# Third block of a two-block transformer pair: the MLP's up products split into two halves of 256 tokens

## The chip, the cores and the metric

The kernel runs on one core of one Trainium2 chip. The metric is the device time of one execution in microseconds (us). A core has engines that run side by side, each with its own instruction queue: TensorE (PE; its weight loads are shown apart as PEld), VectorE (DVE), ScalarE (ACT), GpSimd (POOL) and SyncE (SP), which here only issues DMAs. They wait for each other on semaphores.

## The reference

The input `x` is 32 sequences of 128 tokens by 512 features, float32. Two layers follow each other; the second is cut here to what matters:

```python
    def _L1_cond_ref(x, cond, ...):
        ...
        x_in = x
        h = film(rmsnorm(x, norm1_w), cond, film1_w, film1_b)
        Q = h @ q_w + q_b
        K = h @ k_w + k_b
        V = h @ v_w + v_b
        scores = jnp.einsum('bnd,bmd->bnm', Q, K) * D ** (-0.5)
        attn = jax.nn.softmax(scores, axis=-1)
        out = jnp.einsum('bnm,bmd->bnd', attn, V)
        x = x_in + (out @ proj_w + proj_b)
        x_in = x
        h = film(rmsnorm(x, norm2_w), cond, film2_w, film2_b)
        h = jax.nn.gelu(h @ mlp_w1 + mlp_b1, approximate=False) @ mlp_w2 + mlp_b2
        return x_in + h
```

Before it, layer 0 is an attention with 16 heads between two conditioned layer norms. The change touches `h @ mlp_w1` alone: 4096 tokens by 512 features, times a 512 by 2048 weight.

## The kernel before

The program has three blocks, one after the other on every engine: layer 0 (to about 568 us), the attention half of layer 1 (to about 847 us), and the MLP half of layer 1, the third block, to the end. Tokens are worked in tiles of `P` = 128 and groups of `GB` = 4 tiles, so `GT` = 512 tokens and `NG` = 8 groups. The helper `groups` (line 71) writes a block's body for the first group, once more as a hardware loop over the six groups between, and for the last.

Products of float32 values are made of rounded operands. A value is split into a high part, rounded to the type float32r, and a low part, the rounded rest; `split_product` (lines 567 to 571) issues three matmuls for one product: high by high (L569), high by low (L570) and low by high (L571). Its second and third arguments are the stationary operand, which PE loads as weights ahead of each matmul, and the next two are the one that streams through. All of them add into one PSUM bank of 128 partitions by 512 columns.

In the third block the streaming operand of an up product is the normed input of a group, `hc_hi` and `hc_lo`, features on partitions and 4 chunks (`C`) of 512 tokens each. These two tiles lie where the second block had `hb_hi` and `hb_lo`, and the trace shows them under those names; the weights `w1_hi` and `w1_lo` are `w_hi` and `w_lo` in it, and `g_hi`, `g_lo` are the gelu's result. Names behind the arrow stand in the order streamed, loaded: `bank<-hb_hi,w_hi` is an up matmul, `bank<-w_hi,g_hi` a down matmul.

PE's order is written out by hand in `body_c`. For each group `g` it runs `FT` = 16 up products `up(g, f)`, each 4 chunks x 3 = 12 matmuls, into `bank[f % 2]`. From the fourth on, each is followed by a down product `down(g, f - LAG)` of the piece three before (`LAG` = 3), also 12 matmuls, 3 for each of the four token tiles, into banks 2 to 5. Three down products are left over at the end of a group; into the first two of them `norm_c` puts eight transposes of the next group's tokens (L970). ACT applies the gelu to each up bank (L1257), and DVE splits its result into `g_hi` and `g_lo`.

The next group's `hc_hi` and `hc_lo` are made from the transposes: tiles 0 and 2 by DVE (L1658, L1663, L1280), tiles 1 and 3 by ACT (L1052, L1245), with the low halves of all four on DVE, in the order 0, 1, 2, 3. Each low half raises the semaphore `clo` by one. `body_c` waits for `clo` to reach `GB * g` before `up(g, 0)`. Each up product ends with one count of `up_done`, for which ACT's gelu waits; PE waits for `gelu_done` before it writes a bank again.

Of the kernel before, what the change touches and what calls it, by code (L numbers as in the profile page):

```python
# [11 lines left out]
P = 128  # L12
D = 512
C = D // P
NB = 32
GB = 4
GT = GB * P
# [19 lines left out]
def wait(engine, sem, value):  # L37

    if isinstance(value, int) and value <= 0:
        return  # L40
    engine.wait_ge(sem, value)
# [37 lines left out]
def block_pair_kernel(nc, xt, cond_t, cols_d, bp0_d, bv0_d, pb1_d, b2_d, wg_t, wb_t, wqkv, wp0,  # L79
                      film1, film2, wq1_t, wk1_t, wv1_t, wp1, w1, w2, out):  # L80
    with ExitStack() as ctx:
# [140 lines left out]
        w1_hi = run("w1_hi", [P, C, FF], F32R)  # L222
        w1_lo = run("w1_lo", [P, C, FF], F32R)
# [4 lines left out]
        hc_hi, hc_lo, xc, xnc = hb_hi, hb_lo, xb, xnb  # L228
# [17 lines left out]
        bank = [ctx.enter_context(nc.psum_tensor(f"bank{i}", [P, D], F32)) for i in range(8)]  # L246
# [14 lines left out]
        def sem(name):  # L261
            return ctx.enter_context(nc.semaphore(name))
# [59 lines left out]
        chi_act, chi_dve, clo = sem("chi_act"), sem("chi_dve"), sem("clo")  # L322
# [243 lines left out]
        def _(pe):  # L566
            def split_product(dst, w_hi, w_lo, a_hi, a_lo, start, stop):

                nc.tensor.matmul(dst, w_hi, a_hi, start=start, stop=False)  # L569
                nc.tensor.matmul(dst, w_hi, a_lo, start=False, stop=False)  # L570
                return nc.tensor.matmul(dst, w_lo, a_hi, start=False, stop=stop)  # L571
# [3 lines left out]
            for k in range(C):  # L575
                if k % 2 == 0:
                    pe.wait_ge(wgb_in[k // 2], 32)
                for i in range(2):
                    tile = 2 * (k % 2) + i
                    last = nc.tensor.matmul(ps_s[0][NB * tile:NB * (tile + 1), :], cond[:, k, :], wgb[:, i, k, :],  # L580
                                            start=(k < 2), stop=(k >= 2))
# [3 lines left out]
            for c in range(C):  # L585
                last = nc.tensor.transpose(ps_s[1][:, c * P:(c + 1) * P], fv0[:, c * P:(c + 1) * P], ident[:])
# [13 lines left out]
            for i in range(2):  # L600
                for c in range(C):
                    last = nc.tensor.transpose(ps_t[i][0:NB, c * P:(c + 1) * P], st_flat[:, i * C + c, :], ident[:])
# [165 lines left out]
            for t in range(NB):  # L768
                g, b = t // GB, t % GB
# [81 lines left out]
            for c in range(C):  # L851
                last = nc.tensor.transpose(bank[3][:, c * P:(c + 1) * P], uc_rows[:, c * P:(c + 1) * P], ident[:])
# [46 lines left out]
            def transpose_pb(g, b):  # L899
                t = GB * g + b  # L900
                pe.wait_ge(bexp, t + 1)
                wait(pe, bpt, 2 * (t - 1))
                nc.tensor.transpose(ps_t[b % 2][:, 0:P], pb[:, b % 2, :], ident[:]).then_inc(btp, 1)

            def attend_b(g, b):
                t = GB * g + b
                pe.wait_ge(bpt, 2 * t + 2)
                pe.wait_ge(bg_free[0], bank_uses_b(g, 4 + 2 * b) + 1)
                wait(pe, x2_ready, t - 1)
                split_product(bank[6 + b % 2][:], ptb_hi[:, b % 2, :], ptb_lo[:, b % 2, :], vb_hi[:, b, :],  # L910
                              vb_lo[:, b % (GB - 1), :], True, True).then_inc(bpv, 1)
# [51 lines left out]
            def norm_c(g, b):  # L963

                t = GB * g + b
                pe.wait_ge(cxn, t + 1)

                wait(pe, ct_free_act if b % 2 else ct_free_dve, 2 * g + b // 2)
                for c in range(C):
                    last = nc.tensor.transpose(bank[6 + b % 2][:, c * P:(c + 1) * P], xnc[:, b, c * P:(c + 1) * P],  # L970
                                               ident[:])
                last.then_inc(ct_full, 1)
# [5 lines left out]
            def up(g, f):  # L978
                n = FT * g + f
                wait(pe, gelu_done, n - 1)  # L980
                for k in range(C):
                    last = split_product(bank[f % 2][:], w1_hi[:, k, f * P:(f + 1) * P], w1_lo[:, k, f * P:(f + 1) * P],
                                         hc_hi[:, k, :], hc_lo[:, k, :], k == 0, k == C - 1)
                last.then_inc(up_done, 1)

            def down(g, f, first):
                n = FT * g + f
                if first and f % 2 == 0:
                    pe.wait_ge(w2_hi_made, f // 2 + 1)
                    pe.wait_ge(w2_lo_made, f // 2 + 1)  # L990
                pe.wait_ge(g_hi_ready, n + 1)
                pe.wait_ge(g_lo_ready, n + 1)
                if f == 0:
                    wait(pe, y_ready, GB * g)
                for b in range(GB):
                    tok = slice(b * P, (b + 1) * P)
                    last = split_product(bank[2 + b][:], g_hi[:, f % (LAG + 1), tok], g_lo[:, f % (LAG + 1), tok],
                                         w2_hi[:, f, :], w2_lo[:, f, :], f == 0, f == FT - 1)
                    if f == FT - 1:
                        last.then_inc(acc_done, 1)  # L1000
                if f < FT - 1:
                    last.then_inc(down_done, 1)

            def body_c(g, first, last):

                if first:
                    pe.wait_ge(blo, NB + GB)
                wait(pe, clo, GB * g)
                if first:

                    pe.wait_ge(w1_hi_made, 2 * C - 2)
                    pe.wait_ge(w1_lo_made, 2 * C - 2)
                for f in range(FT):
                    if first and f == FT // 2:
                        pe.wait_ge(w1_hi_made, 2 * C)
                        pe.wait_ge(w1_lo_made, 2 * C)
                    up(g, f)
                    if first and f == 0:
                        transpose_pb(NG - 1, GB - 1)
                    if first and f == 1:  # L1020
                        attend_b(NG - 1, GB - 1)
                    if f >= LAG:
                        down(g, f - LAG, first)
                if first:
                    pe.wait_ge(x2_ready, NB)
                for f in range(FT - LAG, FT):
                    if not last and f < FT - LAG + 2:
                        for b in range(2):
                            norm_c(g, 2 * (f - (FT - LAG)) + b)
                    down(g, f, first)  # L1030

            groups(pe, body_c)


# [844 lines left out]
```

## Time and profile before

| | |
|---|---|
| median of 3 runs | 1560.82 us (1558.15 to 1561.24) |
| the profiled execution | 1561.84 us, its span 1560.1 us |
| mean granted TensorE clock | 0.995 |
| PE busy | 1524.7 us, 98% of the span, 8992 matmuls |
| PE weight loads (PEld) | 1237.5 us, 79%, beside the matmuls |
| DVE, ACT, POOL busy | 786.5, 597.0, 578.1 us |

The span is the time from the first to the last instruction that the profile shows. PE's busy time counts pipelined matmuls, which overlap each other: a matmul of 0.39 us may be followed by the next after 0.23 us. So the distance from start to start, not the length, tells what one costs. The clock is given as a share of full speed, 1.00 being 2.4 GHz.

### The profile page before, as it was taken

Reading aid. Unit: us, or ns where it says so; the run is one execution under the profiler, and the core shown is the slowest. Engines: PE = TensorE matmul, PEld = TensorE weight load, DVE = VectorE, ACT = ScalarE, POOL = GpSimd, SP = SyncE. Lnnn points to the kernel's source line nnn. Section 1 sums busy time; section 2 is a strip of 40 time slices with the busy share of each in tenths; the row PEclk is TensorE's granted clock in tenths of the full one; section 3 lists DMA queues with packets and bytes.
Section 4 is the critical chain, followed back from the end, with each engine's and each line's share of the span. In section 5 each row is a group of like instructions: output and inputs, shape, how many; then the busy total and the mean of one; then the engine's idle time right before and its main releaser. Section 6 shows DMA issues by size and latency. Waiting matters only on the chain.

```text
span 1560.1 us, 25120 instructions
## 1 busy us (share of the span) xinstructions
PE 1524.7 (98%) x8992; PEld 1237.5 (79%) x8992; DVE 786.5 (50%) x1616; ACT 597.0 (38%) x1884; POOL 578.1 (37%) x504
## 2 busy tenths in 40 slices
PE   5999999999999998999999999999999999999999
PEld 3888888888887666778787888888888888888887
DVE  5667777777776665444546533242423324242522
ACT  4656565655543444555555321121212212121210
POOL 5666666767553534443333402121120202121100
PEclk9999999999999999999999999999999999999999
DMA  7122222222216234222223402020101102020100
GB/s 248 62 80 85 82 89 92 79 96 69 81 56 239 88 113 161 84 81 87 87 101 144 147 1 82 0 74 7 67 13 46 34 0 81 0 74 7 54 1 28
DMA packets 56577, 117.72 MB, mean 75 GB/s; under 512 B 6288, under 2 KB 6288, under 8 KB 55984
## 3 DMA queue, kind: packets, MB, share of 16 engines
q1 hardware_dynamic: 56496, 116.65, 21.8%
q8 instruction: 49, 0.80, 0.2%
q14 instruction: 32, 0.26, 0.1%
HBM read 91.33 MB, written 25.30 MB: 75 GB/s over the span
## 4 chain that ended last, share of the span: by engine, by line
PE 91%; DMA 3%; DVE 2%; ACT 1%; POOL 1%; issue 1%; SPq 1%; ACTq 0%; DVEq 0%; POOLq 0%
PE bank L569 26%; PE bank L571 25%; PE bank L570 25%; PE bank L648 4%; PE bank L641 2%; PE bank L659 2%; PE bank L944 1%; PE bank L691 1%; PE bank L593 1%; DMA xb<-x_dram 1%; PE bank L970 1%; PE bank L700 1%; DMA xa<-xt_in 1%; ACT hb_new L1052 1%; POOL xa L1733 1%
## 5 line engine op out<-in xcount | busy, mean ns | idle before, releaser
L1257 ACT ACTIVATE gf<-bank,cols 128x512 f32<-128x512 f32 x128 | 88.3, 690 | 513.2 <-PE bank L571 513.1
L1692 DVE CAST g_hi<-gf 128x512 fp32r<-128x512 f32 x128 | 67.7, 529 | 426.5 <-ACT gf L1257 426.4
L1092 ACT ACTIVATE pa<-bank,neg_max 128x128 f32<-128x128 f32 x512 | 181.7, 409 | 135.0 <-DVE neg_max L1364 135.0
L569 PE MATMUL bank<-w_hi,g_hi 128*128 128x512 f32 x512 | 200.5, 392 | 0.0
L569 PE MATMUL bank<-hb_hi,w_hi 128*128 128x512 f32 x512 | 199.4, 389 | 0.6 <-issue 0.6
L571 PE MATMUL bank<-w_hi,g_lo 128*128 128x512 f32 x512 | 199.4, 389 | 0.0
L570 PE MATMUL bank<-w_lo,g_hi 128*128 128x512 f32 x512 | 199.2, 389 | 0.0
L571 PE MATMUL bank<-hb_hi,w_lo 128*128 128x512 f32 x512 | 199.2, 389 | 0.0
L570 PE MATMUL bank<-hb_lo,w_hi 128*128 128x512 f32 x512 | 199.2, 389 | 0.0
L1742 POOL TENSOR_TENSOR xrc<-xrc,b 128x512 f32<-128x512 f32 x32 | 48.1, 1533 | 302.6 <-DMA xrc<-x_dram 302.6
L1768 POOL TENSOR_TENSOR pa<-pa,rec 128x512 f32<-128x512 f32 x128 | 132.2, 1041 | 49.8 <-DVE rec L1387 49.7
L1757 POOL TENSOR_TENSOR rstd<-ve,neg_half 128x1 f32<-128x1 f32 x64 | 41.0, 640 | 283.9 <-DVE ve L1446 283.9
L1092 ACT ACTIVATION_READ_ACCUMULATOR pa<-bank,neg_max 128x1 f32 x512 | 126.9, 248 | 0.0
L569 PEld LDWEIGHTS bank<-hb_hi,w_hi 128*128 128x128 f32 x512 | 96.1, 188 | 20.9 <-issue 1.0
L571 PEld LDWEIGHTS bank<-w_hi,g_lo 128*128 128x128 f32 x512 | 96.1, 188 | 20.1
L571 PEld LDWEIGHTS bank<-hb_hi,w_lo 128*128 128x128 f32 x512 | 96.1, 188 | 20.0
L570 PEld LDWEIGHTS bank<-hb_lo,w_hi 128*128 128x128 f32 x512 | 96.1, 188 | 19.9
L570 PEld LDWEIGHTS bank<-w_lo,g_hi 128*128 128x128 f32 x512 | 96.2, 188 | 19.5
L569 PEld LDWEIGHTS bank<-w_hi,g_hi 128*128 128x128 f32 x512 | 96.2, 188 | 19.4
L1364 DVE TENSOR_REDUCE neg_max<-bank 128x4 f32<-128x512 f32 x128 | 83.5, 679 | 45.6 <-PE bank L641 45.6
L1280 DVE TENSOR_TENSOR g_lo<-gf,g_hi 128x512 fp32r<-128x512 f32 x128 | 98.5, 770 | 4.4
L1760 POOL TENSOR_SCALAR xnb<-xb,rstd 128x512 f32<-128x512 f32 x60 | 94.9, 1582 | 11.4 <-issue 7.0
(201 smaller groups left out, 3162.3 us busy)
## 6 DMA issues: line engine op xcount, KB each, us to landing
rows<-st_dram SPq DMA_DIRECT2D x32, 512.0 KB, 4.1
xb<-x_dram SPq DMA_DIRECT2D x60, 256.0 KB, 3.3
xa<-xt_in SPq DMA_DIRECT2D x32, 256.0 KB, 4.2
xra<-xt_in SPq DMA_DIRECT2D x32, 256.0 KB, 2.7
x_dram<-h SPq DMA_DIRECT2D x32, 256.0 KB, 2.0
xrb<-x_dram SPq DMA_DIRECT2D x32, 256.0 KB, 3.6
x_dram<-xrb SPq DMA_DIRECT2D x32, 256.0 KB, 2.0
xrc<-x_dram SPq DMA_DIRECT2D x32, 256.0 KB, 3.8
```

The source lines that it names most:

```text
L569: nc.tensor.matmul(dst, w_hi, a_hi, start=start, stop=False)
L570: nc.tensor.matmul(dst, w_hi, a_lo, start=False, stop=False)
L571: return nc.tensor.matmul(dst, w_lo, a_hi, start=False, stop=stop)
L648: last = nc.tensor.transpose(scores_bank[j][:, m * P:(m + 1) * P], pa[:, j, m, :], ident[:])
L1092: last = nc.scalar.activation(pa[:, j, m, :], scores_bank[j][:, m * P:(m + 1) * P], ACT.Exp, bias=neg_max[:, j * C + m:j * C + m + 1], acc ...
L1257: nc.scalar.activation(gf[f % 2][:], bank[f % 2][:], ACT.Gelu, bias=cols[:, B1_COL + f:B1_COL + f + 1])\
L1280: return nc.vector.tensor_tensor(dst, whole, high.bitcast(F32), ALU.subtract)
L1364: nc.vector.tensor_reduce(neg_max[:, j * C:(j + 1) * C], scores_bank[j][:].rearrange("p (h k) -> p h k", h=C), AX.X, ALU.max, negate=True) ...
L1692: nc.vector.tensor_copy(g_hi[:, r, :], gf[f % 2][:]).then_inc(g_hi_ready, 1)
L1742: nc.gpsimd.tensor_tensor(x[:, i], x[:, i], row[:], ALU.add).then_inc(ready, 1)
L1760: nc.gpsimd.tensor_scalar(xn[:, slot], x[:, i], rstd1[:, i:i + 1], None, ALU.mult).then_inc(ready, 1)
L1768: nc.gpsimd.tensor_tensor(pa[:, j], pa[:, j], rec[:, j * C:(j + 1) * C].unsqueeze(2).broadcast_to([P, C, P]), ALU.mult)\
```

## The change

Each up product is written as two halves of 256 tokens (`tok`), with all 12 matmuls of the first half ahead of those of the second. A half has its own start and stop flags on its own 256 columns of the bank. The weight slices are the same in both halves and are loaded for each. In a group's first product (`f == 0`) each half has its own wait on `clo`: the first for `GB * g - 2`, the first two token tiles of the group, the second for `GB * g`. The wait ahead of the whole group is gone.

```diff
             def up(g, f):
                 n = FT * g + f
                 wait(pe, gelu_done, n - 1)
-                for k in range(C):
-                    last = split_product(bank[f % 2][:], w1_hi[:, k, f * P:(f + 1) * P], w1_lo[:, k, f * P:(f + 1) * P],
-                                         hc_hi[:, k, :], hc_lo[:, k, :], k == 0, k == C - 1)
+                for i in range(2):
+                    if f == 0:
+
+                        wait(pe, clo, GB * g - GB // 2 + i * GB // 2)
+                    tok = slice(i * GT // 2, (i + 1) * GT // 2)
+                    for k in range(C):
+                        last = split_product(bank[f % 2][:, tok], w1_hi[:, k, f * P:(f + 1) * P],
+                                             w1_lo[:, k, f * P:(f + 1) * P], hc_hi[:, k, tok], hc_lo[:, k, tok],
+                                             k == 0, k == C - 1)
                 last.then_inc(up_done, 1)
...
                 if first:
                     pe.wait_ge(blo, NB + GB)
-                wait(pe, clo, GB * g)
                 if first:
```

On PE, the start of the looped group body before, with the jump into the loop ahead of it:

```order
L571 MATMUL bank<-w_hi,g_lo 128x512
L74 UNCONDITIONAL_BRANCH
L74 ISA
L41 ISA [waits clo]
L569 MATMUL bank<-hb_hi,w_hi 128x512 [waits gelu_done]
L570 MATMUL bank<-hb_lo,w_hi 128x512
L571 MATMUL bank<-hb_hi,w_lo 128x512
L569 MATMUL bank<-hb_hi,w_hi 128x512
```

and the same place now, with the beginning of the second half further down:

```order
L571 MATMUL bank<-w_hi,g_lo 128x512
L74 UNCONDITIONAL_BRANCH
L74 ISA
L41 ISA [waits gelu_done]
L569 MATMUL bank<-hb_hi,w_hi 128x256 [waits clo]
L570 MATMUL bank<-hb_lo,w_hi 128x256
L571 MATMUL bank<-hb_hi,w_lo 128x256
...
L569 MATMUL bank<-hb_hi,w_hi 128x256 [waits clo]
L570 MATMUL bank<-hb_lo,w_hi 128x256
L571 MATMUL bank<-hb_hi,w_lo 128x256
```

Nothing moved past anything else: 12 rows of 512 columns became 24 rows of 256, and the wait on `clo` stands now at the 1st and the 13th of them. The other 15 products of a group became 24 rows each in the same way, without `clo`. The order of ACT, DVE, POOL and SP is as before.

## Rows read from the trace of the kernel before

**Rows 1.** The page: busy times of the engines, and the chain by line.

```profile
PE 1524.7 (98%) x8992; PEld 1237.5 (79%) x8992; DVE 786.5 (50%) x1616; ACT 597.0 (38%) x1884; POOL 578.1 (37%) x504
...
PE bank L569 26%; PE bank L571 25%; PE bank L570 25%; PE bank L648 4%; PE bank L641 2%; PE bank L659 2%; PE bank L944 1%; PE bank L691 1%; PE bank L593 1%; DMA xb<-x_dram 1%; PE bank L970 1%; PE bank L700 1%; DMA xa<-xt_in 1%; ACT hb_new L1052 1%; POOL xa L1733 1%
```

**Rows 2.** Busy time by engine in the third block (x: instructions).

```profile
core 0: us, PE busy (x) PEld busy (x) DVE busy (x) ACT busy (x) POOL busy (x), PEclk, DMA share, GB/s
846.60:1560.00 713.40, 710.18 (x3188) 588.81 (x3188) 248.92 (x430) 146.13 (x267) 114.87 (x95) 1.00 0.12 40
```

**Rows 3.** All waits of PE from 846 us to the end.

```profile
engine line waited for: us in total, times, longest us
PE bank L569 <- issue: 0.6, 1, 0.6
```

**Rows 4.** Timeline at the first boundary between groups (start us, length us).

```profile
929.78 0.69 DVE L1280 TENSOR_TENSOR hb_lo<-hfc_act,hb_hi 128x512 fp32r<-128x512 f32 x1
...
933.39 0.69 DVE L1280 TENSOR_TENSOR hb_lo<-hfc_act,hb_hi 128x512 fp32r<-128x512 f32 x1
...
936.19 0.39 PE L571 MATMUL bank<-w_hi,g_lo 128*128 128x512 f32 x1
936.19 0.19 PEld L569 LDWEIGHTS bank<-hb_hi,w_hi 128*128 128x128 f32 x1
936.42 0.39 PE L569 MATMUL bank<-hb_hi,w_hi 128*128 128x512 f32 x1
```

**Rows 5.** Timeline at the last boundary: fourth low half, first up matmul.

```profile
1466.49 0.69 DVE L1280 TENSOR_TENSOR hb_lo<-hfc_act,hb_hi 128x512 fp32r<-128x512 f32 x1
...
1469.35 0.39 PE L571 MATMUL bank<-w_hi,g_lo 128*128 128x512 f32 x1
1469.58 0.39 PE L569 MATMUL bank<-hb_hi,w_hi 128*128 128x512 f32 x1
```

**Rows 6.** Timeline of PE: one up product, from down to down.

```profile
949.79 0.39 PE L571 MATMUL bank<-w_hi,g_lo 128*128 128x512 f32 x1
950.02 0.39 PE L569 MATMUL bank<-hb_hi,w_hi 128*128 128x512 f32 x1
...
952.51 0.39 PE L571 MATMUL bank<-hb_hi,w_lo 128*128 128x512 f32 x1
952.74 0.39 PE L569 MATMUL bank<-w_hi,g_hi 128*128 128x512 f32 x1
```

**Rows 7.** Groups by line and form (busy us, mean ns): the up products.

```profile
L569 PE MATMUL bank<-hb_hi,w_hi 128*128 128x512 f32 x512 | 199.4, 389 | 0.6 <-issue 0.6
...
L571 PE MATMUL bank<-hb_hi,w_lo 128*128 128x512 f32 x512 | 199.2, 389 | 0.0
L570 PE MATMUL bank<-hb_lo,w_hi 128*128 128x512 f32 x512 | 199.2, 389 | 0.0
```

**Rows 8.** The chain in order of time (start us, us): unrounded operands. L691 streams 512 columns.

```profile
54.52 1.10 PE bank L641 x32
...
489.92 3.43 PE bank L691 x8
...
630.90 0.89 PE bank L944 x8
...
926.60 0.87 PE bank L970 x8
```

**Rows 9.** Timeline of the weight loads around L944, 128 columns, and after.

```profile
630.63 0.97 PEld L944 LDWEIGHTS bank<-hb,tb 128*128 128x128 f32 x8
631.52 0.30 PEld L947 LDWEIGHTS bank<-inv_hd,rb 128*128 128x128 f32 x2
631.77 0.19 PEld L569 LDWEIGHTS bank<-wvp_hi,hb_hi 128*128 128x128 f32 x1
631.87 0.19 PEld L570 LDWEIGHTS bank<-wvp_lo,hb_hi 128*128 128x128 f32 x1
```

**Rows 10.** Timeline: the last matmul ahead of a pause of PE.

```profile
592.36 0.39 PE L570 MATMUL bank<-vb_lo,ptb_hi 128*128 128x512 f32 x1
592.36 0.19 PEld L571 LDWEIGHTS bank<-vb_hi,ptb_lo 128*128 128x128 f32 x1
592.58 0.39 PE L571 MATMUL bank<-vb_hi,ptb_lo 128*128 128x512 f32 x1
...
598.09 0.48 PE L903 MATMUL bank<-ident,pb 128*128 128x128 f32 x1 [5.12 <-ACT pb L1219]
```

**Rows 11.** Timeline of PE in the first block, other engines at work beside.

```profile
302.64 0.40 PE L570 MATMUL bank<-wv_lo,h_hi 128*128 128x512 f32 x1
302.88 0.40 PE L571 MATMUL bank<-wv_hi,h_lo 128*128 128x512 f32 x1
...
304.96 0.39 PE L571 MATMUL bank<-wv_hi,h_lo 128*128 128x512 f32 x1
```

## Prediction

> **What bounds the kernel now.** I read the page first: TensorE (PE) is busy for 1524.7 of 1560.1 us, and three code lines, L569 to L571, carry 76% of the chain that ended last [rows 1]. They are the three matmuls of `split_product`, so the question is only what the third block spends in them and in the waits between them. Then I read the stages: the third block runs from 846.6 us to the end, and in its 713.4 us PE is busy for 710.2 at a granted clock of 1.00, while VectorE (DVE) is busy for 249 and ScalarE (ACT) for 146 [rows 2]. That is 2.4 GHz throughout. Then the waits of PE inside that stretch: one row, 0.6 us, at its very beginning [rows 3]. The reader should see in this list what is missing from it: no wait for `hb_lo` or `hb_hi` (under whose names the trace shows `hc_lo` and `hc_hi`) at any of the seven later group starts.
>
> The boundary between two groups shows why. DVE ends the second token tile's low half at 929.78 + 0.69 = 930.47 us and the fourth's at 933.39 + 0.69 = 934.08. PE is meanwhile in the last down products, and the first up matmul of the next group starts at 936.42, 0.23 us behind the matmul before it, as everywhere else [rows 4]. So `clo` is complete 2.3 us before PE asks for it. The last boundary reads the same: 1467.18 against 1469.58 us, 2.4 us [rows 5]. The seven boundaries lie 88.9 us apart with the same picture.
>
> **The change part by part.**
>
> (a) The wait on all four token tiles becomes one on two, and the other two are waited for half a product later. It would let PE start up to 934.08 - 930.47 = 3.6 us earlier, if PE stood there. It doesn't stand, so the saving is 7 x 0 = 0. The two new waits cost nothing either by the same rows: matmuls that carry waits (the first of each up and down product) follow their predecessors at the same 0.23 us [rows 4, 6]. Behind the second wait stand twelve matmuls of the first product's second half, and nobody new waits for them, since `up_done` is still raised once, by the last matmul. If the slack of 2.3 us were gone, the wait would be worth having; it is a cover that the kernel does not need now.
>
> (b) Every up product, not only a group's first, now issues 24 matmuls of 256 columns in place of 12 of 512, each with its own weight load. There are 8 groups x 16 products x 12 = 1536 matmuls (512 in each of three rows) [rows 7], so 3072 after. All lie on PE, the bound, with no cover. Everything hangs on one price, the time from one matmul to the next at 256 columns, which no row shows, as every product of rounded operands in this trace is 512 wide.
>
> What 512 columns cost: one up product takes 952.74 - 950.02 = 2.72 us, 226.7 ns a matmul [rows 6]. Its 1536 matmuls make 348 us. The halves break even at 113.3 ns each, and each nanosecond above that costs 3.07 us.
>
> The lower bound comes from the unrounded operands, whose records stream each column twice. Records of 128 columns follow each other in 0.87 / 8 = 109 ns, those of 512 columns in 3.43 / 8 = 429 ns [rows 8]. The difference is 320 ns for 384 columns, 0.833 ns a column, thus 0.417 ns for one pass (2.4 GHz), and about 2.4 ns are left for each record. So 512 rounded columns would need 213.3 ns at that rate, and take 13.4 ns more. A half needs 106.7 ns plus a share of these 13.4 ns, and the three answers are: no share but the 2.4 (109), half (113.4), or all of it (120).
>
> Weight loads set a floor too. Their rows say 0.19 us each, more than a half's stream, but they overlap: the eight matmuls of L944, each with a load of that length, take 0.89 us, 111 ns each, and their loads start as often [rows 8, 9]. So a load per 111 ns is sustained; the floor for a half is 111 to 112 ns, and 113.3 just clears it. The gain has its bound there: 3072 x 1.6 = 5 us at 111.7 ns, and at 109 ns, if these loads went as fast as those of the transposes, 13 us.
>
> Which share? Two rows speak for half. First, the excess does not come from the load: the last matmul before PE's pause of 5.1 us has no load beside it, and is as long (0.39 us) as those that have one [rows 10]. So doubling the loads need not double it. Second, where DVE, ACT and DMAs work beside it, the same kind of matmul takes longer than 227 ns (302.64 to 304.96 us: ten steps of 232 ns on average, single ones of 240) [rows 11]: the stream is slowed while it runs, in proportion to its length, rather than paying at its start. Against it: the 2.4 ns of the other rows are paid once per instruction, and the whole excess could be. I take 113.3 ns, the half share: 3072 x 113.3 - 348 = 0 us.
>
> The Trainium skill, "TensorE: Matmul & The Clock Gate", section "Back-to-back issue gap", puts the warm distance at N/2.4 + 2.5 ns, a fixed part per matmul. By it, halving costs 2.5 ns a pair, an estimate of 3.8 us in all. The 109 and 429 ns of rows 8 agree with it, the 226.7 ns of rows 6 do not (it gives 215.8).
>
> (c) The instruction stream of PE grows: 192 more matmuls with their loads per group of 89 us. The product's 24 matmuls in 2.72 us are 9 per us; L641 runs 32 in 1.10 us, three times denser, so neither issue nor fetching limits [rows 8]. Other engines keep their order; ACT's gelu starts when a product's last matmul ends, as before. Cost 0.
>
> The sum: 0 + 0 + 0 on the profiled execution, 1560.1 us of span and 1561.8 us with what lies around it; the median of the runs is 1560.8. I predict **1561 us**.
>
> **The rivals.** "Faster", "same" and "slower" are divided at 0.2% (3.1 us), which is about what a measurement of this kernel can tell from no change. That is 1.0 ns on each half: it decides from 114.3 ns upward and 112.3 ns downward.
>
> Rival A, slower: the 13.4 ns are a fixed price per matmul of rounded operands. Halves take 106.7 + 13.4 = 120 ns, 1536 x 13.4 = +20.6 us, 1581 us. For it: all matmuls in the quiet stretch show exactly the same 226.7 ns, as a constant would. Against it: rows 11, where it isn't constant.
>
> Rival B, a little slower: a fixed 2.4 ns [rows 8] and the other 11 ns by length. Halves take 106.7 + 2.4 + 5.5 = 114.6 ns, 1536 x 2.4 = +3.7 us, 1564.5 us. For it: the same 2.4 ns appear at both widths of the unrounded records. Against it: if reading the operand is what slows the stream, it goes on reading across the gap between two matmuls and the 2.4 ns are hidden in it. (By its fixed part per matmul, the Trainium skill's rule named above comes nearest to this rival.)
>
> Rival C, much slower: a load of rounded weights does not overlap the load before it, and a half takes the load's 188 ns. 3072 x 188 - 348 = +229 us. Against it: rows 9 show a rounded load begun 0.10 us before the next one (631.77, 631.87). A mild form, where loads back to back need 125 ns or so, would give +36 us.
>
> Rival D, faster: the excess belongs to long streams and halves run at the floor of 111.7 ns, -5 us, 1556 us; at 109 ns -13 us, 1548 us. For it: nothing but the unrounded records. Against it: the load floor.
>
> Rival E, the early start itself gains, as the change's wording suggests. It could only shorten a wait at a group start, and the stretch has none [rows 3]; I give it no chance of its own.
>
> **How the numbers follow.** Forecast (within 0.2%): 0.50. Rival A 0.20, B 0.17 (just beyond the line, slower), C in both forms 0.03, D 0.10. Faster 0.10, same 0.50, slower 0.40. The range leaves out C and the deeper half of D, and takes in A with a margin of 1 us and the shallow half of D: 1555 to 1582 us. The likeliest case alone would span 1558 to 1564.
>
> **What would show it.** In the profile after, one up product of 24 matmuls is the measure: 2.72 us (forecast), 2.75 (B), 2.88 (A), 2.68 or less (D). The loads' starts show the floor: they should follow 0.11 us apart. The boundaries should stay free of waits, with the last low half about 2.3 us ahead of the first up matmul, and down products should stay at 2.72 us. The prediction is wrong if the half's distance is off 113.3 ns by more than 1 ns, if PE shows waits of some us at group starts, or if the clock of the third block leaves 1.00.

## The result and the profile after

The changed kernel takes 1581.83 us (median of 4 runs, 1580.79 to 1583.54) against 1560.66 us (4 runs): 21.2 us or 1.4% longer, ratio 1.014 with a 95% interval of 1.0122 to 1.0157. I had forecast no change, 1561 us. The time lies at the upper end of my range and on the price of rival A (1581 us), to which I had given 0.20.

The page of the profile after, the lines that answer to [rows 1] (busy times, clock in tenths over 40 slices, chain by line):

```profile
span 1581.8 us, 28192 instructions
...
PE 1549.3 (98%) x10528; PEld 1318.2 (83%) x10528; DVE 784.3 (50%) x1616; ACT 596.6 (38%) x1884; POOL 579.0 (37%) x504
...
PEclk9999999999999999999999999999999999999999
...
PE bank L569 26%; PE bank L570 25%; PE bank L571 25%; PE bank L648 3%; PE bank L641 2%; PE bank L659 2%; PE bank L944 1%; PE bank L691 1%; DMA xb<-x_dram 1%; PE bank L970 1%; PE bank L700 1%; PE bank L593 1%; DMA x_dram<-xrb 1%; DMA xra<-xt_in 1%; DMA wgb<-wb_t_in 0%
```

PE has 10528 - 8992 = 1536 matmuls more, as counted, and DVE, ACT and POOL are as busy as before. The clock did not fall: its mean is 0.998, against 0.995 before. The waits of PE from 840 us on, and the busy time of the third block, answer to [rows 2, 3]:

```profile
PE bank L569 <- issue: 0.6, 1, 0.6
PE bank L569 <- DVE ptb_lo L1285: 0.2, 1, 0.2
...
846.60:1581.00 734.40, 731.88 (x4720) 668.02 (x4719) 245.72 (x429) 145.48 (x264) 115.15 (x95) 1.00 0.12 39
```

Still no wait at a group start (the 0.2 us belong to the second block). At the first boundary the fourth low half ends at 936.07 us and the first up matmul starts at 938.38, so the slack is 2.3 us as before. The block lasts 21 us longer than the 713.4 us of [rows 2], and PE is busy all through it. So the time is in the matmuls themselves. The timeline of PE shows where: the end of an up product, one down product, one up product, and the next down (start us, length us).

```profile
955.39 0.28 PE L571 MATMUL bank<-hb_hi,w_lo 128*128 128x256 f32 x1
955.51 0.40 PE L569 MATMUL bank<-w_hi,g_hi 128*128 128x512 f32 x1
955.75 0.40 PE L570 MATMUL bank<-w_lo,g_hi 128*128 128x512 f32 x1
...
958.26 0.28 PE L569 MATMUL bank<-hb_hi,w_hi 128*128 128x256 f32 x1
958.37 0.28 PE L570 MATMUL bank<-hb_lo,w_hi 128*128 128x256 f32 x1
958.49 0.28 PE L571 MATMUL bank<-hb_hi,w_lo 128*128 128x256 f32 x1
958.61 0.28 PE L569 MATMUL bank<-hb_hi,w_hi 128*128 128x256 f32 x1
...
961.01 0.28 PE L571 MATMUL bank<-hb_hi,w_lo 128*128 128x256 f32 x1
961.13 0.40 PE L569 MATMUL bank<-w_hi,g_hi 128*128 128x512 f32 x1
```

The up product takes 961.13 - 958.26 = 2.87 us for 24 matmuls: the first follows after 0.11 us, all others after 0.12. Before it was 2.72 us [rows 6]. Times 128 products, 19.5 us. The down product between, whose code did not change, takes 958.26 - 955.51 = 2.75 us instead of 2.72. Its first matmuls behind the halves are spaced 0.24 and 0.23 us, and only the later ones 0.227; 104 of the 128 down products stand behind an up product, so this adds about 3 us. Together 22 to 23 us, against 21.7 between the two spans (1581.8 and 1560.1) and 21.2 between the medians.

### The profile page after: what moved, and what is told of

It reads as the page before. It is cut to its first block, busy times and chain, and to the rows that moved or that the text cites. A ratio compares the mean times of both kernels' runs of the same rounds, so it can differ in the third digit from the quotient of the medians.

```text
span 1581.8 us, 28192 instructions
## 1 busy us (share of the span) xinstructions
PE 1549.3 (98%) x10528; PEld 1318.2 (83%) x10528; DVE 784.3 (50%) x1616; ACT 596.6 (38%) x1884; POOL 579.0 (37%) x504
## 4 chain that ended last, share of the span: by engine, by line
PE 90%; DMA 3%; DVE 2%; ACT 2%; POOL 1%; issue 1%; SPq 0%; ACTq 0%; DVEq 0%; POOLq 0%
PE bank L569 26%; PE bank L570 25%; PE bank L571 25%; PE bank L648 3%; PE bank L641 2%; PE bank L659 2%; PE bank L944 1%; PE bank L691 1%; DMA xb<-x_dram 1%; PE bank L970 1%; PE bank L700 1%; PE bank L593 1%; DMA x_dram<-xrb 1%; DMA xra<-xt_in 1%; DMA wgb<-wb_t_in 0%
## 5 line engine op out<-in xcount | busy, mean ns | idle before, releaser
L569 PE MATMUL bank<-hb_hi,w_hi 128*128 128x256 f32 x1024 | 289.4, 283 | 0.6 <-issue 0.6
L571 PE MATMUL bank<-hb_hi,w_lo 128*128 128x256 f32 x1024 | 289.8, 283 | 0.0
L570 PE MATMUL bank<-hb_lo,w_hi 128*128 128x256 f32 x1024 | 289.7, 283 | 0.0
L1697 DVE CAST g_hi<-gf 128x512 fp32r<-128x512 f32 x128 | 64.3, 502 | 449.8 <-ACT gf L1262 449.4
L569 PEld LDWEIGHTS bank<-hb_hi,w_hi 128*128 128x128 f32 x1024 | 196.1, 192 | 5.1 <-issue 1.0
L570 PEld LDWEIGHTS bank<-hb_lo,w_hi 128*128 128x128 f32 x1024 | 196.2, 192 | 4.1
L571 PEld LDWEIGHTS bank<-hb_hi,w_lo 128*128 128x128 f32 x1024 | 196.1, 192 | 0.0
```

Of the source, the lines that this page charges most:

```text
L1697: nc.vector.tensor_copy(g_hi[:, r, :], gf[f % 2][:]).then_inc(g_hi_ready, 1)
```

## The experiments

Each kernel is an edit of the kernel before or of the changed one. The theories at the start: **T1**, rival A, each matmul of rounded operands pays 13.3 ns whatever its width; **T2**, two rounded weight loads can't follow each other in less than 120 ns, and the stream pays by width; **T3**, the waits and the group starts cost the time. Distances below are from one matmul's start to the next. Where no interval is given, a time is that of a single run.

**One part alone: only the first product of a group in halves, with the two waits** (e1_first_only).

```diff
-                for i in range(2):
+                for i in range(2 if f == 0 else 1):
...
-                    tok = slice(i * GT // 2, (i + 1) * GT // 2)
+                    tok = slice(i * GT // 2, (i + 1) * GT // 2) if f == 0 else slice(0, GT)
```

> Only the first up product of each group is written in halves, with its two waits; the other 15 stay 512 columns wide. Theory T1 (each matmul of rounded operands pays 13.3 ns whatever its width): 8 x 12 = 96 extra matmuls, +1.3 us, 1562 us; no wait at the group starts, as before. Theory T3 (the time comes from the new waits and the group starts, not from the narrow matmuls): nearly all of the 21 us stays, about 1581 us.

Measured: 1560.23 against 1558.92 us (12 and 23 runs), ratio 1.0012 (1.0000 to 1.0024), that is +1.3 us, with an interval from 0 to 3.7 us. T3, which asked for about 1581 us, falls. The waits and the early start are worth nothing here. For the 96 extra matmuls the trace is finer than the medians: from a group's first up matmul to its first down matmul it shows 11.06 us instead of 10.88, which is 8 x 0.18 = 1.4 us, as T1 says.

**The other part alone: halves everywhere, one wait in front** (e2_one_wait).

```diff
                 for i in range(2):
-                    if f == 0:
-
-                        wait(pe, clo, GB * g - GB // 2 + i * GB // 2)
...
                 if first:
                     pe.wait_ge(blo, NB + GB)
+                wait(pe, clo, GB * g)
```

> All up products in halves as in the changed kernel, but with the single wait on all four token tiles in front of the group. T1: 1581.8 us, the same as the changed kernel, halves 120 ns apart. T3 (the two waits cost the time): back to about 1561 us.

Measured: 1580.2 us, ratio 1.0144 (1.0126 to 1.0163), +21.3 us. The whole loss is in the halves.

**Unequal parts, 384 and 128 columns** (e3_384_128), to tell a price per matmul from a floor of the load. The edit on e2_one_wait:

```diff
-                    tok = slice(i * GT // 2, (i + 1) * GT // 2)
+                    tok = slice(0, 3 * P) if i == 0 else slice(3 * P, GT)
```

> Up products in two unequal parts of 384 and 128 columns, one wait in front. T1 (fixed price per matmul): 160 + 13.3 = 173 ns and 53.3 + 13.3 = 67 ns, 240 ns a pair as with equal halves, about 1582 us. Theory T2 (120 ns is the shortest distance of two rounded weight loads, and the stream itself pays by length): the part of 384 takes 170 to 173 ns, the part of 128 is held at 107 to 120 ns, a pair 280 to 293 ns, 1536 x (53 to 66) = 82 to 102 us more than before, 1643 to 1663 us.

Measured: 1653.78 us, ratio 1.061 (1.059 to 1.063), +95 us. The timeline of one up product, at the change from one width to the other:

```profile
982.78 0.33 PE L571 MATMUL bank<-hb_hi,w_lo 128*128 128x384 f32 x1
982.95 0.33 PE L569 MATMUL bank<-hb_hi,w_hi 128*128 128x384 f32 x1
983.13 0.33 PE L570 MATMUL bank<-hb_lo,w_hi 128*128 128x384 f32 x1
983.30 0.33 PE L571 MATMUL bank<-hb_hi,w_lo 128*128 128x384 f32 x1
983.47 0.22 PE L569 MATMUL bank<-hb_hi,w_hi 128*128 128x128 f32 x1
983.53 0.27 PE L570 MATMUL bank<-hb_lo,w_hi 128*128 128x128 f32 x1
983.64 0.27 PE L571 MATMUL bank<-hb_hi,w_lo 128*128 128x128 f32 x1
...
984.65 0.28 PE L571 MATMUL bank<-hb_hi,w_lo 128*128 128x128 f32 x1
984.76 0.45 PE L569 MATMUL bank<-w_hi,g_hi 128*128 128x512 f32 x1
```

384 columns take (983.47 - 982.78) / 4 = 173 ns: 160 + 13.3, so T1's price is there. 128 columns take (984.76 - 983.53) / 11 = 112 ns: a load floor, which T1 had left out, but at the 111 to 112 ns of the prediction and not at T2's 120. The total and both distances lie inside the bounds that I had allowed to T2 (+82 to 102 us, 170 to 173 and 107 to 120 ns), so the bounds were too wide to decide. What refutes T2 is its premise: loads that follow each other in 112 ns can't be what holds a half at 120. The first 128-column matmul, whose load ran beside a long stream, takes only 0.06 us (60 ns in the trace). That is under the floor, and also under 53.3 + 13.3 = 66.7 ns.

**Halves with 64 weight columns** (e4_64_cols); half of the output features are left out. The edit on e2_one_wait:

```diff
-                        last = split_product(bank[f % 2][:, tok], w1_hi[:, k, f * P:(f + 1) * P],
-                                             w1_lo[:, k, f * P:(f + 1) * P], hc_hi[:, k, tok], hc_lo[:, k, tok],
+                        last = split_product(bank[f % 2][0:64, tok], w1_hi[:, k, f * P:f * P + 64],
+                                             w1_lo[:, k, f * P:f * P + 64], hc_hi[:, k, tok], hc_lo[:, k, tok],
```

> Halves of 256 columns, but with 64 weight columns loaded instead of 128, so that a load is half as long; leaves out half of the output features of each up product. T1: the stream's price doesn't depend on the load, halves stay 120 ns apart, 1582 us. T2 (the load's length sets the 120 ns): halves fall to the stream's own 107 to 113.3 ns, 0 to -18 us against before, 1543 to 1561 us.

Measured: 1563.24 us, ratio 1.0028 (1.0014 to 1.0041). The first and the last matmuls of one up product:

```profile
961.24 0.28 PE L569 MATMUL bank<-hb_hi,w_hi 128*64 128x256 f32 x1
...
963.86 0.28 PE L571 MATMUL bank<-hb_hi,w_lo 128*64 128x256 f32 x1
963.97 0.40 PE L569 MATMUL bank<-w_hi,g_hi 128*128 128x512 f32 x1
```

2.73 us for 24, almost all at 113.3 ns. So the price of a half does depend on what is loaded beside it: half the load, half the price. T1 expected 120 ns, and as "whatever else happens" it is not the whole truth. 113.3 ns is the upper end of what T2 expected, but T2 had fallen with e3. The kernel still takes 4.3 us more than before, though its halves cost what full widths did: the up products make about 1 us of it, and the 104 down products behind them, at 2.75 us, about 3. I formed **T4**: a load takes time from the stream in proportion to its columns.

**Full width with fewer weight columns** (e5_512_64_cols, e9_512_32_cols), on the kernel before; the second is the same with 32 for 64.

```diff
-                    last = split_product(bank[f % 2][:], w1_hi[:, k, f * P:(f + 1) * P], w1_lo[:, k, f * P:(f + 1) * P],
+                    last = split_product(bank[f % 2][0:64, :], w1_hi[:, k, f * P:f * P + 64], w1_lo[:, k, f * P:f * P + 64],
```

> Up products 512 tokens wide as before, but with 64 weight columns loaded instead of 128; leaves out half of the output features. Theory T4 (a rounded weight load takes time from the stream in proportion to its columns, 13.3 ns for 128 and 6.7 ns for 64): 213.3 + 6.7 = 220 ns, an up product of 2.64 us, 1536 x 6.7 = 10 us less than before. Theory T2 (halves were held at 120 ns by the length of a load, wide streams pay by their own width): nothing changes at 512 columns, 226.7 ns and 2.72 us, the time of before.

> The same with 32 weight columns; leaves out three quarters of the output features. T4: 213.3 + 3.3 = 216.7 ns, an up product of 2.60 us, or a floor of about 2.4 ns per matmul if it is larger; 15 us less than before. T2: 2.72 us, unchanged.

Measured: 1566.32 us (ratio 1.0045, 1.0029 to 1.0062) and 1572.57 us, beside 1558.33 of the kernel before. Both became slower, by 8 and 14 us, where T4 said 10 and 15 us faster. T4 falls. In e5 the distances no longer stand at 227 ns but run through 236, 229, 224, 227, 234, 230, mean 230; in e9 through 231, 234, 229, 233, mean 232.

**Every third load narrow** (e8_mixed_loads), an edit of e2_one_wait:

```diff
                     for k in range(C):
-                        last = split_product(bank[f % 2][:, tok], w1_hi[:, k, f * P:(f + 1) * P],
-                                             w1_lo[:, k, f * P:(f + 1) * P], hc_hi[:, k, tok], hc_lo[:, k, tok],
-                                             k == 0, k == C - 1)
+                        w = P if k == C - 1 else 64
+                        nc.tensor.matmul(bank[f % 2][:, tok], w1_hi[:, k, f * P:(f + 1) * P], hc_hi[:, k, tok],
+                                         start=(k == 0), stop=False)
+                        nc.tensor.matmul(bank[f % 2][:, tok], w1_hi[:, k, f * P:(f + 1) * P], hc_lo[:, k, tok],
+                                         start=False, stop=False)
+                        last = nc.tensor.matmul(bank[f % 2][0:w, tok], w1_lo[:, k, f * P:f * P + w],
+                                                hc_hi[:, k, tok], start=False, stop=(k == C - 1))
```

> Halves of 256 columns in which every third matmul (low weights by high inputs) loads 64 columns and the other two 128, except in a half's last chunk; leaves out part of the low weights' product. It tells whose load a matmul pays for. T4a (it pays for the load that runs beside it, the next matmul's): the matmul ahead of the narrow load takes 113.3 ns, the other two 120. T4b (it pays for taking over its own weights): the matmul with the narrow load takes 113.3 ns, the other two 120. T2 (a floor by the length of a load): 113.3 ns ahead of the narrow load as in T4a, so this run separates T4b alone.

Measured: 1576.64 us. Mean distance 117.5 ns, but no matmul stands out at 113 as asked: the distances mix between 113 and 125. It decides nothing between T4a and T4b, the two forms of T4; the delays are not booked matmul by matmul, as both had assumed.

**Halves of bfloat16 operands** (e7_bf16_halves), an edit of e2_one_wait; the products' values are left out.

```diff
+                iw = ident[:].bitcast(BF16)
...
-                        last = split_product(bank[f % 2][:, tok], w1_hi[:, k, f * P:(f + 1) * P],
-                                             w1_lo[:, k, f * P:(f + 1) * P], hc_hi[:, k, tok], hc_lo[:, k, tok],
-                                             k == 0, k == C - 1)
+                        last = split_product(bank[f % 2][:, tok], iw[:, 0:P], iw[:, 0:P], iw, iw, k == 0, k == C - 1)
```

> Halves of 256 columns with bfloat16 operands from one constant tile; leaves out the up products' values. T4 in its form that the 4-byte operands' reads collide: bfloat16 takes half of the reads, and a half falls to 106.7 + 2.4 = 109 ns, an up product of 2.62 us. If the price belongs to any load of 128 columns: 120 ns, 2.88 us.

Measured: 1552.53 us.

```profile
964.29 0.27 PE L569 MATMUL bank<-ident 128*128 128x256 bf16 x1
...
964.73 0.27 PE L570 MATMUL bank<-ident 128*128 128x256 bf16 x1
964.84 0.27 PE L571 MATMUL bank<-ident 128*128 128x256 bf16 x1
```

(964.84 - 964.29) / 5 = 110 ns; over the inner matmuls of the product, 109. Only about 2.4 of the 13.3 ns remain. This is the first of the prediction's three answers, "no share but the 2.4", for a type that the kernel doesn't use. The run doesn't show that the type alone does it: both operands also come from one small constant tile here, and the run that would tell, rounded operands from that tile, was not made. The kernel gains little by it, since the down product behind such halves takes 2.85 us instead of 2.72.

**Which fetch pays: one column repeated** (e13_stream_one_column, e14_load_one_column), at full width. The first repeats the streamed column, the second the loaded one:

```diff
-                                         hc_hi[:, k, :], hc_lo[:, k, :], k == 0, k == C - 1)
+                                         hc_hi[:, k, 0:1].broadcast_to([P, GT]), hc_lo[:, k, 0:1].broadcast_to([P, GT]),
+                                         k == 0, k == C - 1)
```

> Up products 512 wide with full weights as before, but the streaming operand is one column repeated 512 times; leaves out the values of all other tokens. Theory T5 (the 13.3 ns above the stream's own 213.3 are spent in fetching the streaming operand from SBUF): 216 ns, an up product of 2.59 us. If they are spent in fetching or taking over the weights, or in the array: 226.7 ns, 2.72 us, unchanged.

> Up products 512 wide, but all 128 weight columns are one column repeated; leaves out the values of all other weight columns. Theory T6 (the 13.3 ns are spent where the fetch of the weights crosses that of the stream): 216 to 220 ns, 2.59 to 2.64 us. T5 and any price of taking the weights over: 226.7 ns, 2.72 us, unchanged.

Measured: 1546.12 us and 1566.95 us, beside 1559.15. The timeline of e13:

```profile
960.68 0.38 PE L569 MATMUL bank<-hb_hi,w_hi 128*128 128x512 f32 x1
...
963.05 0.38 PE L571 MATMUL bank<-hb_hi,w_lo 128*128 128x512 f32 x1
963.27 0.39 PE L569 MATMUL bank<-w_hi,g_hi 128*128 128x512 f32 x1
```

2.59 us for 12, 216 ns each. With the same instructions, the same loads and the same type, 11 of the 13.3 ns are gone once the streamed operand needn't be fetched column by column. T5 holds against what it was tested against, a price of taking over the weights or of the array: the excess is there only where the stream reads different columns. e14 went the other way, to a mean of 231 ns, so T6, that one repeated weight column would relieve the fetch, falls; but what the loads read does move the stream's time. So whether the stream's fetch pays alone, or by meeting the loads' fetch, stays open. In e13 the down products behind take 2.76 us, although the width didn't change.

**The same in halves, and a fourth width** (e15_halves_stream_one, e16_halves_load_one, e17_320_192). The edits are those of e13 and e14 made on e2_one_wait, and for e17:

```diff
-                    tok = slice(i * GT // 2, (i + 1) * GT // 2)
+                    tok = slice(0, 320) if i == 0 else slice(320, GT)
```

> Halves of 256 columns, one wait, full weight loads, but the streaming operand is one column repeated; leaves out the values of all other tokens. T5 (fetching the streaming operand costs the time, in halves too): 109 to 112 ns a half, an up product of 2.62 to 2.69 us, a time at or below the kernel before's. Load floor at 120 ns: 2.88 us, as in the changed kernel.

> Halves of 256 columns, one wait, all 128 weight columns one column repeated; leaves out the values of the other weight columns. If the price depends on where the loads read beside the stream, it moves away from 120 ns, as the full width's moved from 226.7 to 231; if halves have a fixed price, 120 ns and 2.88 us.

> Up products in parts of 320 and 192 columns, one wait. Fixed 13.3 ns per matmul: the part of 320 takes 133.3 + 13.3 = 146.7 ns. Price by width: 133.3 + 8.3 = 141.7 ns. The part of 192 takes 80 + 13.3 = 93.3 ns if only the stream counts, and about 112 ns if the load floor of the 128-wide parts holds it.

Measured: 1554.58, 1576.46 and 1610.01 us, beside 1559.2. First e15, then e17:

```profile
962.12 0.27 PE L569 MATMUL bank<-hb_hi,w_hi 128*128 128x256 f32 x1
...
964.69 0.28 PE L571 MATMUL bank<-hb_hi,w_lo 128*128 128x256 f32 x1
964.80 0.40 PE L569 MATMUL bank<-w_hi,g_hi 128*128 128x512 f32 x1
```

```profile
962.03 0.31 PE L569 MATMUL bank<-hb_hi,w_hi 128*128 128x320 f32 x1
...
962.77 0.31 PE L571 MATMUL bank<-hb_hi,w_lo 128*128 128x320 f32 x1
962.91 0.25 PE L569 MATMUL bank<-hb_hi,w_hi 128*128 128x192 f32 x1
963.00 0.28 PE L570 MATMUL bank<-hb_lo,w_hi 128*128 128x192 f32 x1
...
964.23 0.41 PE L569 MATMUL bank<-w_hi,g_hi 128*128 128x512 f32 x1
```

e15: 2.68 us for 24, 112 ns each. So the floor of a rounded 128-column load is 112 ns, as the prediction had it, and not 120: the changed kernel's halves stand 8.4 ns above the floor, and these go when the stream reads one column. e17: (962.91 - 962.03) / 6 = 147 ns for 320 columns, the fixed price, and (964.23 - 963.00) / 11 = 112 ns for 192, the floor. The first of the 192-column matmuls, behind wider ones, takes 0.09 us (88 ns in the trace, where 80 + 13.3 would be 93.3). So the 13.3 ns are the price inside a row of equal matmuls; the first one behind wider ones pays about 7 to 8. e16 took 116.7 ns a half on average, neither 120 nor 113.

**If the slack at the group start were gone** (e10_late_one_wait, e11_late_first_halves). The transposes of the next group are moved back, in e10 on the kernel before, in e11 on e1_first_only:

```diff
                 for f in range(FT - LAG, FT):
-                    if not last and f < FT - LAG + 2:
+                    if not last and f == FT - LAG + 1:
                         for b in range(2):
-                            norm_c(g, 2 * (f - (FT - LAG)) + b)
+                            norm_c(g, b)
                     down(g, f, first)
+                if not last:
+                    for b in range(2, GB):
+                        norm_c(g, b)
```

> The kernel before, with the transposes of the next group one and two places later (tiles 0 and 1 ahead of the middle one of the three last down products' successor, tiles 2 and 3 behind the last one), so that the cover of the group start is gone. Both theories: DVE ends the fourth low half 4.0 us after the second transposes begin, so PE waits about 3.2 us at each of seven group starts; up to 7 x 3.2 = +22 us, 1583 us. It is the base for the next run.

> The same late transposes, but a group's first up product in halves with their two waits. T1 to T4 alike (the early start is worth something only where PE stands at the group start): the first half, 1.4 us, runs while the third and fourth tile are still being made, so 7 x 1.4 - 1.3 = 9 us less than the run before, about 1574 us. Against it: if the second half's wait only moves the standstill, without shortening it, the two are equal.

Measured: 1585.13 us (ratio 1.0166, 1.0149 to 1.0183) and 1573.36 us (1.0091, 1.0074 to 1.0108), beside 1559.3. The waits of PE in the third block, e10 and then e11 (us in total, times, longest):

```profile
PE bank L569 <- DVE hb_lo L1283: 21.4, 7, 3.1
```

```profile
PE bank L569 <- DVE hb_lo L1288: 10.9, 7, 1.6
```

Here the early start does what it is meant for: each of the seven waits is 1.5 us shorter, as the first half of 12 matmuls, 1.4 us, runs in it. The medians differ by 11.8 us, against the 9 expected, but part of that is clock: three of the five runs of e10 (1585 to 1589 us) had a mean granted clock of 0.990 to 0.992, the other two, at 0.997, took 1583.1 and 1583.3. Against e11, at 0.996 to 0.999, these two give about 10 us. It needs only the group's first product to be split. Neither kernel reaches the one before, and no run here that keeps the computation whole beats it.

## Why the prediction was wrong

**Held.** Bound and stage: all of the change's time is on PE in the third block. The count, 1536 matmuls more. The saving of zero: no wait stood at the group starts [rows 3], the slack was 2.3 us [rows 4, 5] and still is, and e1 and e2 show both waits to be free. The load floor of 111 to 112 ns [rows 8, 9]: e3, e15 and e17 measured 112. The clock stayed at 1.00. Rival A comes nearest, 1536 x 13.4 = 20.6 us against 21.2 measured, but not by its sum alone: the up products gave 19.5 us, because the first half behind a down product took 0.11 us and not 0.12, and about 3 us came from the down products, which no case of mine had; small changes elsewhere take a little off.

**Failed: "I take 113.3 ns, the half share".** The half takes 120 ns, and 3072 x 120 - 348 is 20.6 us where the sum had 0. The distances of the rounded matmuls with full weight loads, in the steady part of each product, are:

| columns | distance | less columns / 2.4 GHz | from |
|---|---|---|---|
| 512 | 226.7 ns | 13.3 | before |
| 384 | 173.3 ns | 13.3 | e3 |
| 320 | 146.7 ns | 13.3 | e17 |
| 256 | 120.0 ns | 13.3 | the changed kernel |
| 192, 128 | 112 ns | load floor | e17, e3 |

The share is whole at every width above the floor: the 13.3 ns are fixed, not proportional. Two readings led me to a half. From [rows 10] I concluded that the excess doesn't come from the load, since the last matmul ahead of a pause is as long as the others. But the ends of matmuls are modelled in these records, and a length is not a distance: it could not carry that. The page after shows it:

```profile
L571 PE MATMUL bank<-hb_hi,w_lo 128*128 128x256 f32 x1024 | 289.8, 283 | 0.0
```

Halves are 283 ns long and full widths 389 [rows 7]. The difference, 106 ns, is that of 256 columns at 2.4 GHz, and the 13.3 ns that each half pays don't show in it.

From [rows 11] I concluded that other engines at work slow the stream while it runs, and that it must so pay in proportion to its length. The row was misread. Its matmuls are the first twelve behind 32 narrow ones (L641, 301.19 us), and that place accounts for them. The trace before has the same stretch once more with all engines busy (start us, length us; then busy us by engine, clock, DMA share, GB/s):

```profile
470.68 1.17 PE L641 MATMUL bank<-ka,qa 32*128 32x128 f32 x32
...
472.12 0.40 PE L570 MATMUL bank<-wv_lo,h_hi 128*128 128x512 f32 x1
...
474.45 0.39 PE L571 MATMUL bank<-wv_hi,h_lo 128*128 128x512 f32 x1
...
474.90 0.39 PE L570 MATMUL bank<-h_lo,wk_hi 128*128 128x512 f32 x1
...
477.17 0.39 PE L571 MATMUL bank<-h_hi,wk_lo 128*128 128x512 f32 x1
```

```profile
474.90:477.17 2.27, 2.27 (x11) 1.88 (x10) 1.41 (x4) 2.27 (x13) 1.71 (x2) 1.00 0.93 307
931.16:933.01 1.85, 1.85 (x9) 1.50 (x8) 1.78 (x6) 1.80 (x5) 0.00 (x0) 1.00 0.00 0
```

Behind the narrow ones ten distances are (474.45 - 472.12) / 10 = 233 ns. The ten from 474.90 us on are 227 ns, while ACT works all the time, DVE and POOL for most of it, and the DMA engines stand at 0.93. The second window is the reverse: no DMA and no POOL, but eight narrow transposes just ahead, and the eight distances in it are 1.85 / 8 = 231 ns. Over the whole trace before, from the fourteenth matmul of a row of 512-column rounded ones on, all 3386 distances are 226 or 227 ns, whatever else runs. So nothing here spoke for a price by length, and what I held against the constant was no exception to it. That constant, 226.7 ns in all quiet stretches, was in my text as the evidence for the other side, and I weighed it less. One width can't give a slope and an intercept; [rows 8] had two widths, and there the rest was a fixed one.

**Failed too: "down products should stay at 2.72 us".** The sum had no term for them. Behind halves they take 2.75 us, 104 times, about 3 us. It is the pattern of rows 11 again: the first few wide matmuls behind other ones stand further apart.

Rival B's 114.6 ns stand in no run with the kernel's own operands. Its fixed part alone, 2.4 ns, is what is left in the bfloat16 halves (109 ns in e7) and in the rounded stream of one column (216 ns in e13). The Trainium skill ("TensorE: Matmul & The Clock Gate", "Back-to-back issue gap") gives N/2.4 + 2.5 ns. The traces of e7 and e13 agree with it, those of the rounded operands as the kernel uses them don't: 120 ns where it gives 109.2. The Trainium skill also says, on the same page (the section "Step-by-step: what each phase is for"), that loading the next weights doesn't take read bandwidth from the running matmul. No run here measures bandwidth, but the loads do change the stream's time: with nothing but them changed, halves went from 120 to 113.3 ns (e4) and to 116.7 (e16), and full widths from 226.7 to 230, 232 and 231 (e5, e9, e14).

**Open.** Why a matmul whose stream reads different columns costs a fixed 13.3 ns. It depends on what is loaded beside it, but not by the load's columns alone, since fewer columns made the wide stream slower. The distances of e5, e9 and e14 go through short repeating patterns. The down products behind other matmuls take some five to ten of their own to return to 227 ns, and in e13 do so without a change of width; this looks like two fetches falling in and out of step. It is argued, not shown. Layouts of the two operands in SBUF were not tried.

## What to carry over

Before splitting a product to start part of it early, look for the wait: if the consumer never stands at that point in the trace, the split can only cost. Where it does stand there, split only the product that waits (1.3 us for 96 matmuls here), not all of them (21 us for 1536). Before putting a longer distance down to other engines, look at its place in the row: in the trace before, all of them stand among the first thirteen behind other matmuls or a pause. And price a narrower matmul from at least two widths of the same operand type; with one width, the fixed and the proportional reading are both open.

## What the runs showed of the hardware

- Rows of equal matmuls of rounded float32 (float32r) with 128-column loads, at 2.4 GHz: columns / 2.4 + 13.3 ns at 256, 320, 384 and 512 columns, and 112 ns at 128 and 192. The first matmul of a narrower part behind a wider one takes less: 60 ns at 128 columns, 88 at 192, 113 at 256.
- bfloat16 at 256 columns, both operands from one constant tile: 109 ns.
- 11 of the 13.3 ns vanish when the streamed operand is one repeated column (216 ns at 512 columns; at 256 the load floor of 112 ns takes over).
- The load beside a stream changes its time: 64 instead of 128 weight columns give 113.3 instead of 120 ns at 256 columns, but 230 instead of 226.7 at 512.
- Behind narrower matmuls, or a stream of one repeated column, unchanged wide ones take five to ten matmuls until they stand at 226.7 ns again: 0.03 us in all behind halves. Behind that, all 3386 distances of the trace before are 226 or 227 ns, with DMA at 0.93 and all engines busy too.
